# Two cross-attention layers on one core: a ScalarE step of the even units swapped, and the last even unit's gaps reordered

## The reference

```
q = x @ Wq ; k = ctx @ Wk ; v = ctx @ Wv            # 20 heads of 16 channels
p = softmax(q k^T / sqrt(16))                        # over the 77 keys
x = x + merge(p v) @ Wo + bo
```

## Time and profile before

| | |
|---|---|
| median of 3 runs | 944.73 us (940.63 to 945.84) |
| the profiled execution | 941.04 us |
| its span | 939.2 us |
| TensorE busy in the span | 903.8 us |
| VectorE, ScalarE, GpSimd busy | 686.2, 544.1, 400.0 us |

### The profile page before, as it was taken

One profiled execution on the slowest core, in us unless ns is written; L12 is line 12 of the kernel. 1 busy time (PEld: TensorE's weight loads), 2 busy tenths in 40 slices (PEclk: granted clock), 3 DMA queues, 4 the chain that ended last, 5 costly groups with the idle time before them and its releaser, 6 DMA issues.

```text
span 939.2 us, 28086 instructions
## 1 busy us (share of the span) xinstructions
PE 903.8 (96%) x11518; PEld 685.7 (73%) x11518; DVE 686.2 (73%) x1223; ACT 544.1 (58%) x547; POOL 400.0 (43%) x227
## 2 busy tenths in 40 slices
PE   8899999999999999998999999999999999999797
PEld 5777778777777877776677687777778777777564
DVE  4776786867678686686768778786787878677456
ACT  4456565656666565565466656566565656656452
POOL 3433354624435453365443456354344625422223
PEclk9999999999999999999999999999999999999999
DMA  6313434544453544544455444444544544444342
GB/s 212 89 34 93 132 99 113 142 127 132 104 142 90 160 133 120 139 117 121 122 145 140 106 108 128 132 131 123 132 107 110 132 128 133 113 116 98 94 107 84
DMA packets 80526, 112.41 MB, mean 120 GB/s; under 512 B 21200, under 2 KB 37878, under 8 KB 80400
## 3 DMA queue, kind: packets, MB, share of 16 engines
q1 hardware_dynamic: 80400, 110.61, 44.3%
HBM read 60.24 MB, written 22.24 MB: 88 GB/s over the span
## 4 chain that ended last, share of the span: by engine, by line
PE 49%; DMA 17%; SPq 15%; DVE 8%; issue 6%; ACT 3%; POOL 1%; DVEq 0%; ACTq 0%; POOLq 0%
PE pR L306 18%; PE pR L432 8%; PE pA L379 6%; SPq L1389 6%; PE pR L366 5%; DMA X<-y 5%; DMA X<-in_xT 4%; DMA y<-X 4%; PE pR L286 2%; SPq L1359 2%; SPq L1396 2%; DMA out<-X 2%; PE pR L256 2%; SPq L1423 2%; ACT P L742 2%
## 5 line engine op out<-in xcount | busy, mean ns | idle before, releaser
L742 ACT ACTIVATE P<-pA 77x2048 f32<-77x2048 f32 x160 | 300.3, 1877 | 166.8 <-PE pA L385 166.6
L993 DVE TENSOR_REDUCE Mx<-pR 128x4 f32<-128x308 f32 (+1 forms) x480 | 258.9, 575 | 32.7 <-PE pR L366 27.5
L1252 POOL TENSOR_TENSOR On<-On,OS 128x1024 f32<-128x1024 f32 (+1 forms) x58 | 105.7, 1844 | 276.7 <-DMA OS<-rd 276.6
L306 PE MATMUL pR<-OS,Wo 128*128 128x512 f32 x638 | 170.1, 406 | 4.1 <-DVE OS L1049 3.3
L306 PE MATMUL pR<-XS,Wq 128*128 128x512 f32 x638 | 168.5, 403 | 2.7 <-POOL Wq L1238 1.6
L432 PE MATMUL pR<-P,VA 77*17 77x256 f32 x2480 | 156.8, 383 | 2.2 <-DVE Mx L993 1.6
L366 PEld LDWEIGHTS pR<-KH,QH 32*128 32x128 f32 x1280 | 96.5, 183 | 78.2 <-issue 43.7
L366 PE MATMUL pR<-KH,QH 32*128 32x154 f32 x1280 | 132.0, 284 | 15.4 <-ACT P L742 7.4
L379 PE MATMUL pA<-QH,KH 32*77 32x256 f32 x1280 | 145.6, 292 | 0.1
L306 PEld LDWEIGHTS pR<-OS,Wo 128*128 128x128 f32 x638 | 114.7, 189 | 34.6 <-issue 4.8
L306 PEld LDWEIGHTS pR<-XS,Wq 128*128 128x128 f32 x638 | 116.3, 189 | 31.8 <-POOL Wq L1238 2.0
(11 more groups left out here) (154 smaller groups left out, 1215.2 us busy)
## 6 DMA issues: line engine op xcount, KB each, us to landing
On<-Oraw SPq DMA_DIRECT2D x248, 64.0 KB, 2.7
OS<-rd SPq DMA_DIRECT2D x58, 256.0 KB
C<-in_cT SPq DMA_DIRECT2D x16, 616.0 KB, 8.0
X<-in_xT SPq DMA_DIRECT2D x16, 512.0 KB
y<-X SPq DMA_DIRECT2D x16, 512.0 KB, 4.2
X<-y SPq DMA_DIRECT2D x16, 512.0 KB
out<-X SPq DMA_DIRECT2D x15, 512.0 KB, 4.2
X<-in_xT SPq DMA_DIRECT2D x16, 256.0 KB
```

The lines of the kernel that those rows point to most:

```text
L306: f = pe.matmul(p[:, :], W[:, k, c0:c0 + 128], S[:, s, :], start=(i == 0), stop=(i == len(pairs) - 1))
L742: act.activation(P[0:L, i % PR, :, :], pA[0:L, :, :], ACT.Exp, scale=float(D) ** -0.5).then_inc(p_done, 1)
L993: dve.tensor_reduce(Mx[:, :, :].rearrange("p t (j i) -> p j t i", j=4)[:, j:j + banks, :, i:i + 2], pR[:, bank:bank + banks, 0:2 * LK].rea ...
L1252: pool.tensor_tensor(On[rows, blocks, :], On[rows, blocks, :], recips(u, part).bitcast(F32), ALU.mult).then_inc(o_mul, 1)
```

## The change

On ScalarE, in the even units from 2 to 28, `S(u, 1)` and `split_x(u + 2)` change places. In unit 30, all three engines' lists are reordered: TensorE has `Q(31, 2)` and `V(15, 2)` in the first gap in place of `out(28, 1)`, then `out(28, 0)` and `out(28, 1)` in the second gap and `out(28, 2)` in the third. No instruction is added or removed, and no transfer.

```diff
# TensorE, unit 30
                         Q(u + 1, 1, 2)
-                        out(z, 1, 0)
+                        Q(u + 1, 2, 1)
+                        V(w - 1, 2, 0)
                         run(u, 1, n, 2, 0)
                         out(z, 0, 3)
-                        V(w - 1, 2, 0)
+                        out(z, 1, 0)
                         run(u, 2, n, 2, 0)
-                        Q(u + 1, 2, 3)
+                        out(z, 2, 2)
                         PV(u, 0, 1)
                         run(u, 3, n, 2, 0)
-                        out(z, 2, 2)
                         PV(u, 1, 3)
# ScalarE
                 if u % 2 == 0:
-                    split_o(z, 0)
+                    if u < NU - 2:
+                        split_o(z, 0)
                     S(u, 0)
-                    split_o(z, 1)
+                    if u < NU - 2:
+                        split_o(z, 1)
...
                     elif u < NU - 2:
                         K(w, 1)
                         Q(u + 1, 1)
+                        S(u, 1)
                         split_x(u + 2)
-                        S(u, 1)
                         if u < NU - 4:
                             v_half_copy(w)
...
                     else:
+                        split_o(z, 0)
                         Q(u + 1, 1)
+                        v_half_copy(w - 1)
+                        q_half_copy(u + 1)
+                        split_o(z, 1)
                         S(u, 1)
-                        v_half_copy(w - 1)
+                        V_last(2)
                         S(u, 2)
-                        V_last(2)
-                        q_half_copy(u + 1)
                         o_copy(u, 0)
# VectorE, unit 30
+                        Q_lo(u + 1, 1)
+                        V(w - 1, 2)
+                        q_sum(u + 1)
                         split_o(z)
-                        Q_lo(u + 1, 1)
+                        Q_hi(u + 1, 2)
+                        Q_lo(u + 1, 2)
+                        maxima(n, 1, 1, 0, 2)
                         recip_last(v)
                         recip(v)
+                        out(z, 0)
                         out(z, 1)
-                        maxima(n, 1, 1, 0, 2)
-                        out(z, 0)
-                        V(w - 1, 2)
                         maxima(n, 2, 0, 1, 2)
-                        q_sum(u + 1)
+                        out(z, 2)
                         maxima(n, 3, 0, 1, 2)
-                        Q_hi(u + 1, 2)
-                        Q_lo(u + 1, 2)
-                        out(z, 2)
                         maxima(n, 4, 1, 0, 2)
```

## The result

The changed kernel takes 955.05 us (median of 4 runs, 951.06 to 961.21), the kernel before 945.29 us beside it (4 runs, 940.63 to 946.16). The ratio is 1.0115, with a 95% interval of 1.0064 to 1.0167. The profiled execution's span is 955.3 us, 16.1 us more than before.

A forecast was written before the change was run, and what follows sets the result against it. TensorE, busy 903.8 of 939.2 us, was taken to bound the kernel. Later Q starts in even units (+10.5 us net), unit 28's clock (+1.6) and unit 30 (0) made +12.1 on 941.04: 953 us, range 943 to 961.

The forecast's parts named there:

- The total: Whole kernel: 10.5 + 1.6 + 0 = +12.1 us on the profiled execution's 941.04, giving 953.
- What the swap removes: Head of run 2, units 2 to 28: all seven TensorE waits for the exponential, 7.4 us, are gone.
- L - E: Even units: landing of x's transfer minus end of run 1, -1.20 to 1.63 us; positive ones hold the seven waits.
- The new wait: Third block of Q, even units: TensorE waits about 1.2 us for GpSimd's second subtraction, some 13 times, 15 us.
- The sum over the units: Units 2 to 28: new start of Q's third block minus the old, together +10.5 us.
- Units 12 and 14: Unit 12: Q earlier and at the upper clock, -2.0 us; unit 14: Q waiting for second-layer weights, +0.85 us.
- Unit 28: No V in its second gap: TensorE waits 2.6 us at Q, Q +1.7 us, with 1.6 us taken for the clock.
- Unit 30: Two waits, 1.0 and 1.6 us, replace one of 2.89; multiplication 2.2 us later; net 0, bounds -1.9 to +2.2.
- (1): Rival: late transfer landings decide, so the swap gains 0.8 us a unit, 11 us, to about 932; chance 0.07.
- (2): Rival: half the loss fills other waits in later gaps and odd units, +6: 947; chance 0.19 together with (4).
- (3): Rival: clock falls in most even units, 12 x 1.6 us more: 972; chance 0.06.
- (4): Rival: swap has no effect, rounding and exponential being hidden; 941 to 943 with unit 30; chance 0.19 together with (2).

The follow-up runs named there:

- run 0: Not a follow-up run: a numbered stretch inside the kernel's unit 30, not defined further in the text; S(30, 4) began 25.43 us behind its start, 25.54 before.
- e6: Changed kernel with a further GpSimd subtraction between its two in the even units, x's remainder 1.3 to 1.4 us later: 1002.06 us, ratio 1.0604 to the kernel before.
- e7: Kernel before, without the swap, with a further GpSimd subtraction between its two in the even units: 954.97 us, ratio 1.0123.
- e3: Changed kernel with K(w, 2) put ahead of Q(u+2, 2) on TensorE in units 2 to 28: 939.88 us, ratio 0.9953 to the kernel before.
- e5: Kernel before with the swap and K(w, 2) ahead of Q(u+2, 2) in units 2 to 28, unit 30 as before: 936.11 us, ratio 0.9917.
- e4: Kernel before with K(w, 2) put ahead of Q(u+2, 2) in units 2 to 28, without the swap: 940.99 us, ratio 0.9973.

## Why the prediction was right, step by step

- **The total**: the forecast was +12.1 us on a profiled execution. The profiled executions differ by 16.1 us (957.12 against 941.04), the medians by 9.8, and by 12.0 for the swap alone (e1), so the size is met as far as the runs can tell. By terms, the profiles have 9.3 us where 10.5 were forecast, 4.0 behind the Q where 1.6 were, and 2.8 in the rest where 0 was.
- **What the swap removes**: right for the exponential, whose waits at run 2 are all gone, but not for the idle time there. Against the 7.4 us, run 2 idles 3.0 us in units 6, 14 and 28 (0.92, 1.12 and 0.94 us) for a residual sum of VectorE, which run 2 needs as well. The reading that the seven waits lie in the units with a positive L - E was wrong in two: unit 28, at -0.31, had 0.94 us of them, and unit 16, at 0.05, had 0.12 us, which isn't among the seven.
- **The new wait**: right in place, cause and count (13), a little too large in size. The rounding starts 1.82 us behind run 1's end, not 1.96, so the Q is at 7.15 and not 7.3, 1.06 us later than in the earlier trace rows where 1.2 were forecast. The idle time of the profile is 0.86 us of that.
- **The sum over the units**: +10.5 us forecast for run 1's end to Q, 9.3 measured.
- **Behind the Q**: only 1.6 us for the clock were in the sum. The 4.0 us there are 0.1 us in each of ten units, where five matmuls behind an idle time take 1.43 us instead of 1.30, and four larger terms: +2.3 in unit 18 (a long K_lo), +3.2 in unit 28 (a long K_hi and a fall of the clock), -2.0 in unit 14 (no K_hi of 3.64 us and its wait, as before) and -0.6 in unit 12 (no fall of the clock).
- **Units 12 and 14**: unit 12's fall of the clock is gone (1.43 us for the five matmuls, 2.00 in the earlier trace rows); the Q of unit 14 is 0.87 us later, 0.85 forecast.
- **Unit 28**: half right. Q came 1.5 us later (1.7 forecast), but there was no single stall of 2.6: 0.94 us stayed at run 2, for the residual sum, and 1.37 came at Q, and the clock did not fall there. It fell 10 us later, behind two waits for VectorE's maxima. In e1's profile it doesn't fall in unit 28 at all. That the 1.6 us taken for it comes near the truth is luck.
- **Collisions of VectorE and GpSimd**: not in the sum. TensorE waited 3.7 us behind them in the trace after, and 1.9 in unit 14 of the trace before: 1.8 us more, which about made good the 1.2 us that the forecast had too much at the Q. That is luck too.
- **Unit 30**: right. Its two waits were 0.90 and 1.44 us (1.0 and 1.6 forecast), GpSimd's multiplication came 1.5 us later from run 0 on (2.2 forecast), and S(30, 4) began 25.43 us behind run 0's start, against 25.54 before. Alone it measures 0.9999. What the forecast didn't have is the tail behind it, 2.4 us longer in this profile by a fall of the clock (below).
- **Rivals**: (1) fell: in 13 of 14 units the rounding starts right behind the exponential, so no landing decides. (2) fell: behind the Q the units lose 4.0 us more and give nothing back. (3) was wrong for waits of 0.86 us, and its mechanism was seen at longer ones: with 2.2 us (e6) the clock falls in ten of the 14 even units. The length alone doesn't decide it: in e7 four waits at run 2 were 2.1 to 2.3 us long, and those of units 10 and 14 were followed by a fall, those of units 6 and 28 were not. (4) fell with e1, e3 and e6.

The profile after, where the tail of unit 30 shows a fall of the clock (windows):

```profile
913.00:916.00 3.00, 2.87 (x28) 1.40 (x32) 0.69 (x1) 0.82 (x3) 0.00 (x0) 0.52 0.03 6
```

PV(30, 4) and PV(30, 3) took 3.62 us there for the 1.94 of the earlier trace rows, and the lower level lasted 6.8 us, into unit 31. From S(30, 4) to the end this profile takes 44.17 us and the one before 41.76: 2.4 us of the 16.1. The kernel with unit 30's order alone (e2) ran the same stretch at a clock of 1.00, so it isn't this order by itself. But the fall stands at this place, 27.3 to 27.4 us behind the start of run 0, in all three profiles that have both the new order and the swap (after, e3, e6), and in none of the eight others. Each is a single profile, and why the two together bring it is open.

## What to carry to other kernels

A step that can't start until something else lands is best read by two times: how long ahead of its consumer it ends now, and how long the step that is put ahead of it takes. Here 0.8 us of cover met 1.9 us of exponential. To let the exponential go first was worth something only once independent work (K's eight matmuls, 1.15 us) stood in front of the matmul that needed the rounding: the swap is +1.2% without that exchange; with it the kernel is at -0.8% (e5), of which the exchange alone is -0.3% (e4). A wait that is removed can uncover another one behind it, as the residual sums did here. And before anything is done that moves an instruction with SBUF operands on VectorE in time, look at what GpSimd runs beside its new place.

## What the runs showed of the hardware that was not expected

- The cost of a repeated stall isn't linear: a wait of 0.86 us in each even unit went with 12 us in all over the kernel before, one of 2.2 us with 59 us, in part because the granted clock (mean 0.974) fell at ten of them, in part because VectorE's K_hi met GpSimd's multiplication in ten units.
- A pair of VectorE instructions of 0.66 us took up to 3.88 us when GpSimd's multiplication began between 0.4 us ahead of it and 0.26 us behind it; the boundary lay between 0.26 and 0.37 us, about where the second instruction of the pair starts. K_hi, with one SBUF tensor as input, was caught in the same way: 2.65 us for 0.50 in unit 28 of the kernel after, 3.64 in unit 14 of the kernel before.
